# Loads of x moved to ScalarE, constants moved to SyncE, and another order of the pieces on every engine

## The reference, cut to what matters

```python
h = _L0_tok_ref(x, L0_tok_conv_w, L0_tok_conv_b)      # 3x3 depthwise conv, then 8x8 mean pooling
h = h + _L0_attn_ref(_layernorm(h), Wq, bq, Wk, bk)   # one head, values are the tokens themselves
h = h + _L0_ffn_ref(_layernorm(h), ...)               # 2 shared experts + top 2 of 8 routed experts
h = h + _L1_attn_ref(_layernorm(h), ...)              # 8 heads, rotary, 15 compressed keys, a sink
h = h + _L1_ffn_ref(_layernorm(h), W1, b1, W2, b2)    # two lower triangular 128x128 matrices, gelu
```

## Time and profile before

| | |
|---|---|
| median of 3 runs | 1971.06 us (1967.69 to 1986.72) |
| profiled execution, its own time | 2000.31 us |
| its span in the profile | 1998.4 us |
| mean granted TensorE clock | 0.932 of 2.4 GHz |

### The profile page before, as it was taken

The page is one execution under the profiler, slowest core; times in us unless marked ns, Lnnn a source line. Parts: engine busy times, 40 slices in busy tenths (PEclk is TensorE's granted clock), DMA queues, the critical chain, the costliest instruction groups (busy, mean ns, idle before and its releaser), DMA issues.

```text
span 1998.4 us, 42920 instructions
## 1 busy us (share of the span) xinstructions
PE 1700.6 (85%) x14896; PEld 1320.4 (66%) x14896; DVE 1307.9 (65%) x3244; ACT 1070.4 (54%) x2707; POOL 754.4 (38%) x643
## 2 busy tenths in 40 slices
PE   1453888989998989999899999898999999897947
PEld 1443666867677777778676777777776768575624
DVE  2467476878677777568686777777777868442222
...
DMA packets 109125, 331.56 MB, mean 166 GB/s; under 512 B 13662, under 2 KB 87585, under 8 KB 92412
## 3 DMA queue, kind: packets, MB, share of 16 engines
...
## 4 chain that ended last, share of the span: by engine, by line
PE 42%; POOL 19%; DVE 14%; issue 13%; ACT 6%; DMA 4%; ACTq 1%; another core or an unknown queue 0%; SPq 0%; POOLq 0%; DVEq 0%
PE hid_bank L595 7%; POOL yg L1374 7%; PE sec_bank L649 5%; POOL rows_d L1352 5%; PE pool_bank L449 3%; POOL xbuf L1363 3%; PE sec_bank L669 3%; PE sec_bank L660 3%; PE hid_bank L580 3%; PE hid_bank L579 3%; PE pool_bank L454 2%; DVE xc L1268 2%; POOL rs L1335 2%; DVE x L1055 2%; PE hid_bank L581 2%
## 5 line engine op out<-in xcount | busy, mean ns | idle before, releaser
L1363 POOL TENSOR_TENSOR xbuf<-xbuf 128x512 f32<-128x512 f32 x256 | 328.2, 1282 | 633.0 <-DVE xbuf L1063 621.7
L845 ACT ACTIVATE hid<-hid_bank,bias_t 128x128 f32<-128x128 f32 x960 | 273.1, 371 | 116.0 <-PE hid_bank L581 113.6
L595 PE MATMUL hid_bank<-w_s,hid 128*128 x1920 | 291.2, 297 | 0.0
L595 PEld LDWEIGHTS hid_bank<-w_s,hid 128*128 128x128 f32 x1920 | 244.4, 199 | 16.9
L1084 DVE SCALAR_TENSOR_TENSOR taps<-pooled_s,tapw,taps 128x256 f32<-128x256 f32 (+1 forms) x416 | 240.5, 578 | 10.6
L1063 DVE TENSOR_TENSOR xbuf<-xbuf 128x1536 f32<-128x1536 f32 x128 | 224.0, 1750 | 30.4 <-DMA xbuf<-in_x 30.3
L579 PE MATMUL hid_bank<-xt,w_b 128*128 128x128 bf16 x960 | 213.2, 234 | 35.0 <-issue 17.1
L580 PE MATMUL hid_bank<-xt,w_b 128*128 128x128 bf16 x960 | 213.5, 234 | 0.7
L581 PE MATMUL hid_bank<-xt,w_b 128*128 128x128 bf16 x960 | 209.5, 230 | 0.0
L1374 POOL DMA_INDIRECT yg<-outs_d,spot_i x128 | 151.2, 1182 | 54.7 <-issue 38.8
L1067 DVE TENSOR_TENSOR xbuf<-xbuf 128x512 bf16<-128x512 f32 x128 | 102.1, 797 | 98.4 <-ACT xbuf L759 94.6
...
## 6 DMA issues: line engine op xcount, KB each, us to landing
xbuf<-in_x SPq DMA_DIRECT2D x128, 2048.0 KB
...
rows_d<-x2r,spot_i POOLq DMA_INDIRECT x128
yg<-outs_d,spot_i POOLq DMA_INDIRECT x128
```

The source lines that it names most:

```text
L595: mm = nc.tensor.matmul(hid_bank[n % 2][:, 0:P], hid[:, n % RING, q * P:(q + 1) * P], w_q, start=False, stop=q == FC - 1)
L845: ins = nc.scalar.activation(hid[:, n % RING, cols], hid_bank[n % 2][:, cols], ACT.Gelu, bias=bias_t[:, q, j:j + 1])
L1363: nc.gpsimd.tensor_tensor(v[:, :, 1, :], v[:, :, 1, :], v[:, :, 2 * k + 3, :], ALU.add) \
```

## The change

Three things are changed. SyncE issues the constants first and keeps `rows`, `store` and `keep`. ScalarE issues the loads of x as pieces of its own list. The order table is new for every engine, and `setup` is called ahead of the first piece of iteration 1 that isn't a leftover of group 0 or a load (the function `fresh`).

```diff
 ORDER = dict(
     sp="""
-        store.6' store.7' store.4' store.9' store.10' store.8' load.0.0 store.13' store.11' store.12' store.14'
...
+        rows.0' rows.2' store.0' store.1' rows.1' store.4' store.5' store.3' store.2' store.7' store.6' store.8'
...
     pe="""
-        up.0 up.1 table up.2 up.3 down.0 down.1 down.2 up.4 down.3 up.5 out' up.6 down.4 down.5 up.7 pool.0.0
-        pool.0.1 down.6 down.7 pool.0.2 lift.0 att.1 lift.1 widen.0 lift.2 widen.1 att.2 narrow.0 lift.3 pool.0.3
...
+        table pool.3.3' up.0 up.1 down.0 up.2 up.3 down.1 up.4 down.2 up.5 up.6 down.3 up.7 out' down.4 down.5
+        down.6 down.7 pool.0.0 pool.0.1 lift.0 widen.0 lift.1 att.1 lift.2 widen.1 narrow.0 att.2 widen.2
...
+        lift.11 turn.3 att.11 narrow.8 widen.9 value.2 pool.2.2 pool.2.3 turn.4 widen.10 lift.12 value.3 turn.5
+        value.4 narrow.9 turn.6 value.5 lift.13 narrow.10 att.12 value.6 lift.14 turn.7 widen.11 value.7 widen.12
+        post.0 narrow.11 post.1 pool.3.0 widen.13 narrow.12 pool.3.1 widen.14 narrow.13 post.3 pool.3.2 post.4
+        narrow.14 post.5""",
     act="""
...
+        turn.1 lift.9 narrow.6 lift.10 load.3.0 att.10 turn.2 narrow.7 widen.8 inner.2.1 pool.2.0 turn.3 load.3.1
+        lift.11 narrow.8 turn.4 widen.9 turn.5 lift.12 high widen.10 narrow.9 inner.3.0 turn.6 lift.13 narrow.10
...
@@
+        def fresh(g, stage, piece):
+
+            return not (stage == "tok" and (g == 0 or piece[0] == "load"))
@@ SyncE
-            def load(g, u, v):
-                src = x[bass.ds(g * GI + 2 * u, 2), :, v * (HW // 2):(v + 1) * (HW // 2), :]
-                eng.dma_start(xbuf[v][:], src.rearrange("i y x c -> (i y) x c")).then_inc(x_in[v], 16)
-
-            def tokens(g, b, kind, u, v):
-                if u or after(g, 1):
-                    eng.wait_ge(pooled, at(pooled, g, 4 * (u - 1) + 2 * (v + 1)))
-                load(g, u, v)
+            for dst, src in early:
+                eng.dma_start(dst[:], src).then_inc(early_in, 16)
+            for dst, src in loads:
+                eng.dma_start(dst if dst in (limit, place_s, sb2_s, bias_s, before_s) else dst[:], src).then_inc(consts_in, 16)
@@ ScalarE
-            for dst, src in early:
-                eng.dma_start(dst[:], src).then_inc(early_in, 16)
-            for dst, src in loads:
-                eng.dma_start(dst if dst in (limit, place_s, sb2_s, bias_s, before_s) else dst[:], src).then_inc(consts_in, 16)
...
-                if kind == "inner":
+                if kind == "load":
+
+                    if u or after(g, 1):
+                        eng.wait_ge(pooled, at(pooled, g, 4 * (u - 1) + 2 * (k + 1)))
+                    src = x[bass.ds(g * GI + 2 * u, 2), :, k * (HW // 2):(k + 1) * (HW // 2), :]
+                    eng.dma_start(xbuf[k][:], src.rearrange("i y x c -> (i y) x c")).then_inc(x_in[k], 16)
+                elif kind == "inner":
@@ every engine but SyncE
-                if where == 1:
-                    setup()
+                due = where == 1
                 for g, b, stage, piece in pieces(PLAN["act"], i, where):
+                    if due and fresh(g, stage, piece):
+                        setup()
+                        due = False
```

86 lines of the change are left out of this document (43 added, 43 removed).

## The result

The changed kernel takes 2049.91 us (median of 4 runs, 2037.32 to 2070.71) where the kernel before took 1978.89 in the same comparison: a ratio of **1.0333, 95% interval 1.0267 to 1.0398**. It is slower, and lies outside the forecast range. The ratio leaves out the slowest of the four runs, 2070.71 us, which is also the profiled one: its granted clock was 0.875, that of the others 0.880 to 0.892. The profiled execution has a span of 2069.0 us, 70.6 more than that of before.

What follows compares the result with a forecast made beforehand. The period was taken as a GpSimd-set stretch (T to L) plus a TensorE-set stretch (L to T). Gains of 11 us in the fill and 4 in full iterations, less 1 in the drain, gave 1957 us, range 1924 to 1995.

Steps and rivals of the forecast that it cites:

- T to L: From TensorE giving att.12's input (T) to lift.0's start (L), set by GpSimd: 39.1 to 39.0 us, gain 0.1 an iteration.
- L to T: From lift.0's start to the next T, TensorE's own 68.6 us: 1.7 less work, 1.5 new waits, gain 0.2 an iteration.
- The sum: Whole kernel: 11 us of the fill, 4 of the full iterations, 1 lost in the drain: 14 us gained.
- an end of T to L: Slow end of that stretch: pooling pieces at half clock behind an idle stretch add 2.2 us, making T + 40.6.
- rival 1: GpSimd's stretch gets longer: late load.3.1 and half-clock pooling pieces make T to L 41.6; 1990 us; chance 0.20.
- The fill: Kernel start: TensorE begins at 22.0 instead of 33.99; 11 us gained, with 6 and 15 as ends.
- The others that I named: New waits in L to T: widen.7 for the copy of narrow.5, 0.5 us; pre.2 for the gathers' mix, 0 to 1.
- Drain: Last three iterations, without loads of x; narrow.14 one piece later: 1 us lost, between -3 and +4.
- rival 3: The start isn't free: late constants or second load, fill gives 0 to 5 us; 1967 us; chance 0.13.
- Rival 2: The new waits don't come: L to T keeps its 1.7 us, T to L is 37.6; 1918 us; chance 0.22.

Runs made afterwards that it cites:

- old_order: The changed kernel with the order table of the kernel before, loads of x still on ScalarE and constants on SyncE; ratio to before 1.0385.
- sync_loads: The changed kernel with its new order, but SyncE issues the loads of x from group 1 on; ratio to before 1.0543.
- before_cluster: The kernel before with narrow.3 moved behind score.5 on TensorE and its copy on ScalarE behind that of pool.1.3; ratio to before 1.0324.
- rows_first: The changed kernel with the reload rows.1 ahead of the first two stores on SyncE instead of behind them; ratio to before 1.0313.
- fill_only: The kernel before with only the change's start: SyncE issues the constants, ScalarE the eight loads of group 0, setup as in the change; ratio to before 0.9952.

## Why the prediction was wrong, point by point

**The bound.** "The period is a stretch set by GpSimd (T to L) plus a stretch set by TensorE (L to T)" held. What failed is what I put under the second part: "A piece moved out of L to T into T to L is worth its whole length". TensorE's stretch isn't the sum of its pieces, since their order sets the clock at which they run. With four pieces out and two in it became 7.5 us longer.

**The clock.** The failing step is in the first paragraph: the row of the iteration with a clock of 0.84, 10.8 us longer "without waits that would explain it", was read as noise of the execution, "the reason not to forecast from the profiled execution alone". It was the largest number in the rows that bore on this change. The sum has no term for it: half clock appears only as 2.2 us for two pooling pieces, in an end of T to L and in rival 1, and nothing in L to T, where the late falls are. What the runs showed in its place is a loss of 63.0 us in twelve periods by TensorE's longer busy time, with 318 us at half clock against 119; `old_order`, with the loads moved and the order of before, keeps the old clock (113 us), and `sync_loads`, with the new order, has the late falls (212 us). The slow iteration in the rows had 27 us at half clock from T + 86 on. It began in a `narrow`, with no wait of over 0.2 us in the 10 us ahead of it, and why it began isn't tested. `before_cluster` shows that the place of one `narrow` can make late falls the rule. By the Trainium skill (TensorE: Matmul & The Clock Gate, section "What's actually happening") the clock depends on how busy the engine has been; the falls behind waits of 0.8 to 3.7 us in the change agree with that. The falls behind 7.00 us of 7.00 busy in the change, and 7.64 of 8 in `before_cluster`, don't follow from the busy time of the profile, which is modelled; they would need it read as "busy with what", and what that is stays open.

**SyncE's list.** I looked at the constants there and at nothing else. `rows.1` behind `store.1` is a wait that the order alone shows, 2.6 us in each of twelve iterations. It was missing from the sum; `rows_first` shows that it would not have changed the result.

**The fill.** Forecast 11 us (6 to 15), first matmul at 22 us: it was at 22.26, and `fill_only` has its first T 11.0 us sooner and 9.5 us less at the end (0.0048 of 1983; the interval is 2 to 17). In the change it is 18.7 at the first T, and the next two iterations lose 31.2, with clocks of 0.90 and 0.80 where before had 0.98 and 0.94, and 74 us at half clock where before had 17. That loss I didn't foresee.

**T to L.** `scatter.0` at T + 8 (7.55), the root behind the eighth gather, `pool.0.0` waiting 1 to 3 us for the subtraction (0.8 to 2.8), `moe` gone as a releaser: all as walked through. In the iteration shown one gather was slow (2.14 us), where before two were (1.86 and 2.47). The gain was 1.1 us and not 0.1, inside the ends.

**L to T.** Forecast -0.2, measured +7.5. Of the new waits `widen.10` for the copy of `narrow.8` came (0.8 us). The others that I named came to little.

**Drain.** Forecast 1 us lost, measured 18.5 gained. TensorE was at half clock there for 126 us where it was 136, and idle for 57.1 us where it was 68.7. No run tests it, and the cause stays open.

**The rivals.** Rival 1 had the right sign for a wrong reason: T to L got shorter. A sign of it did come, since `pair` pieces waited for x (8.6 us in 12 waits, the longest 1.4, where the kernel before had no such wait), but `scatter.0` came at T + 7.6 in ten of the twelve and at T + 8.5 in two, about as forecast. Against rival 3, `fill_only` has the whole gain at its first T. Rival 2, that L to T keeps its 1.7 us, is in no iteration: the quickest, of 105.8 us and without a late fall, had the 37.3 us from T to L that it says, and 68.5 from L to T, 0.7 less than the mean before.
